# Narrow attention with latents: four evictions and scalings change from VectorE to ScalarE, and GpSimd takes the rows' root ahead of the keys' sum

## The reference, cut to what matters

```python
def mla_attention(x, Wq, Wdkv, Wuk, Wuv, Wo, ln_g, ln_b):
    q = (x @ Wq.T).reshape(b, t, N_HEADS, HEAD_DIM).transpose(0, 2, 1, 3)
    latent = layernorm(x @ Wdkv.T, ln_g, ln_b)
    k = (latent @ Wuk.T).reshape(b, t, N_HEADS, HEAD_DIM).transpose(0, 2, 1, 3)
    v = (latent @ Wuv.T).reshape(b, t, N_HEADS, HEAD_DIM).transpose(0, 2, 1, 3)
    q = apply_rope(q)
    k = apply_rope(k)
    scores = jnp.einsum('bhqd,bhkd->bhqk', q, k) / np.sqrt(HEAD_DIM)
    scores = jnp.where(causal, scores, -jnp.inf)
    attn = jax.nn.softmax(scores, axis=-1)
    out = jnp.einsum('bhqk,bhkd->bhqd', attn, v).transpose(0, 2, 1, 3).reshape(b, t, D_MODEL)
    return out @ Wo.T
x = x + mla_attention(rmsnorm(x, norm1_w), ...)      # x here is a layer norm of the residual
```

## Time and profile before

| | us |
|---|---|
| median of 3 runs (lowest to highest) | 2046.31 (2046.07 to 2053.31) |
| the profiled execution, its own time | 2049.34 |
| its span | 2047.5 |
| busy: TensorE, VectorE, ScalarE, GpSimd | 1493.7, 1348.0, 1172.9, 773.1 |
| mean granted TensorE clock | 0.895 |

### The profile page before, as it was taken

One profiled execution on the slowest core, in us unless ns is written; L12 is line 12 of the kernel. 1 busy time (PEld: TensorE's weight loads), 2 busy tenths in 40 slices (PEclk: granted clock), 3 DMA queues, 4 the chain that ended last, 5 costly groups with the idle time before them and its releaser, 6 DMA issues. The chain is left out here.

```text
span 2047.5 us, 63292 instructions
## 1 busy us (share of the span) xinstructions
PE 1493.7 (73%) x22193; PEld 1111.0 (54%) x22194; DVE 1348.0 (66%) x3733; ACT 1172.9 (57%) x2974; POOL 773.1 (38%) x823
## 2 busy tenths in 40 slices
PE   0688888846888877788424992888888884499991
PEld 0466666624555555556223780566666663377781
DVE  4577777636777777776454664678777875366665
ACT  2366666623544444444433990798888883377770
POOL 0000000022322323231485561336666666466661
PEclk9999999967999999999556995899999996699996
DMA  7110000000001000000012223000011111222227
GB/s 231 32 34 27 31 31 25 26 6 27 31 20 33 21 29 25 26 33 18 23 43 72 74 66 96 12 12 30 29 32 32 31 36 33 79 81 77 81 77 250
DMA packets 110889, 100.81 MB, mean 49 GB/s; under 512 B 17827, under 2 KB 98598, under 8 KB 110656
## 3 DMA queue, kind: packets, MB, share of 16 engines
q1 hardware_dynamic: 87648, 67.02, 11.0%
q0 software_dynamic: 12928, 25.60, 3.8%
q10 hardware_dynamic: 10080, 5.01, 0.8%
HBM read 43.25 MB, written 32.96 MB: 37 GB/s over the span
## 5 line engine op out<-in xcount | busy, mean ns | idle before, releaser
L2497 POOL DMA_INDIRECT e_back<-e_out_rows,e_G x142 | 148.4, 1045 | 98.8 <-issue 56.7
L664 DVE TENSOR_REDUCE m_mx<-m_pM 128x8 f32<-128x1024 f32 x128 | 155.6, 1216 | 29.6 <-PE m_pM L375 29.5
L1459 ACT ACTIVATE w_weights<-w_pS,w_ng 128x77 f32<-128x77 f32 x512 | 157.8, 339 | 17.7 <-DVE w_ng L1547 17.5
L526 ACT ACTIVATE m_PT<-m_pS 128x1024 f32<-128x1024 f32 x128 | 130.4, 1019 | 59.3 <-PE m_pS L404 58.0
L1112 POOL DMA_INDIRECT e_rows<-re_R,re_index x128 | 126.1, 985 | 63.7 <-issue 35.2
L526 ACT ACTIVATE a_PT<-a_pS 77x1024 f32<-77x1024 f32 x128 | 130.5, 1019 | 17.8 <-PE a_pS L404 12.6
L2520 DVE TENSOR_TENSOR e_gl<-e_g,e_gh 128x512 f16<-128x512 f32 x142 | 98.3, 692 | 57.4 <-ACT e_g L2464 53.7
L769 POOL TENSOR_SCALAR a_var<-a_aggr 128x4 f32<-128x4 f32 x16 | 3.1, 193 | 337.0 <-DVE a_aggr L590 337.0
L1660 POOL TENSOR_TENSOR w_weights<-w_weights,w_rec 128x616 f32<-128x616 f32 x64 | 77.9, 1217 | 125.4 <-DVE w_rec L1551 125.0
L664 DVE TENSOR_REDUCE a_mx<-a_pM 128x8 f32<-128x616 f32 x128 | 101.5, 793 | 33.0 <-PE a_pM L375 33.0
L1459 ACT ACTIVATION_READ_ACCUMULATOR w_weights<-w_pS,w_ng 128x1 f32 x512 | 113.6, 222 | 0.0
(11 more groups left out here) (383 smaller groups left out, 5651.1 us busy)
## 6 DMA issues: line engine op xcount, KB each, us to landing
e_G<-e_rows SPq DMA_DIRECT2D x106, 132.0 KB, 2.3
e_B<-e_back SPq DMA_DIRECT2D x16, 512.0 KB, 6.9
stage<-in_split SPq DMA_DIRECT2D x13, 512.0 KB, 4.6
Qs<-a_qh SPq DMA_DIRECT2D x128, 32.0 KB
Qs<-m_qh SPq DMA_DIRECT2D x128, 32.0 KB
Ks<-m_kh SPq DMA_DIRECT2D x32, 128.0 KB
e_R<-e_back SPq DMA_DIRECT2D x16, 256.0 KB, 3.5
w_stage<-in_late SPq DMA_DIRECT2D x16, 256.0 KB, 2.6
```

The lines of the kernel that those rows point to most:

```text
L526: act.activation(PT[:NK, b % 2, 8 * half:8 * half + 8, :], pS[:NK, :, :], ACT.Exp, scale=float(1.0 / np.sqrt(HD))).then_inc(exp_done, 1)
L664: dve.tensor_reduce(out=mx[:, 8 * half:8 * half + 8], in_=pM[:, :, :NK], op=ALU.max, axis=AX.X).then_inc(m_max, 1)
L1459: ac = act.activation(weights[:, b % 2, n, :], pS[:, n // HB, n % HB, :KC], ACT.Exp, bias=ng[:, b % 2, n:n + 1], scale=float(WD) ** -0.5, ...
L2497: pool.indirect_dma_start(out=back, out_offset=bass.IndirectOffsetOnAxis(ap=G[:, r, s, D:D + 1].bitcast(I32), axis=0), in_=out_rows[:, r, ...
```

## The change

Four pieces of work change engine: the scaling of rows by the root (`rms_rows`), the eviction of the values (`part("v")`), gain and bias of the latents (`part("latT")`) and the copy of the turned maxima (`keep_max`). ScalarE used to make `lh` from `lt`; now it makes both from PSUM. On GpSimd the root of the squares stands ahead of the rope of `ks`.

```diff
         @block.scalar
+                elif what == "v" and latent:
+                    act.wait_ge(used, u + 1)
+                    wait(act, pv_ready, lin(g, GB, -GB))
+                    settle(act, c)
+                    for b in range(GB):
+                        cp = act.activation(V[:NK, p, b, :, 0:HD],
+                                            pP[:NK, b * P:(b + 1) * P].rearrange("k (h d) -> k h d", h=H), ACT.Copy)
+                    cp.then_inc(evac, 1)
                 elif what == "latT":
-                    act.wait_ge(evac, u + 1)
-                    act.activation(lh[:], lt, ACT.Copy).then_inc(hi_made, 1)
+                    act.wait_ge(used, u + 1)
+                    wait(act, lat_lo, lin(g, 1, 0))
+                    settle(act, c)
+                    act.activation(lh[:], pP[:LAT, :TG], ACT.Identity, scale=SM("lg", LAT),
+                                   bias=SM("lb", LAT)).then_inc(hi_made, 1)
+                    act.activation(lt, pP[:LAT, :TG], ACT.Identity, scale=SM("lg", LAT),
+                                   bias=SM("lb", LAT)).then_inc(evac, 1)
+            def rms_rows(g):
+                act.wait_ge(ms_done, lin(g, 1, 1))
+                if not is_first(g):
+                    act.wait_ge(lat_lo, lin(g, 1, 0))
+                settle(act, c)
+                for b in range(GB):
+                    act.activation(xn[:, b:b + 1, :], Y[:, bass.ds(lin(g, GB, b), 1), :], ACT.Copy,
+                                   scale=rr[:, b:b + 1]).then_inc(rms_r, 1)
+
+            def keep_max(g, b):
+                act.wait_ge(mt_ready, lin(g, GB, b + 1))
+                wait(act, s_ready, lin(g, 2 * GB, 2 * (b - 1)))
+                act.activation(mT[:, b % 2, :], pTh[:], ACT.Copy).then_inc(mt_kept, 1)
...
             def step(g, p, b, nxt, nxt2):
                 one, two = earlier(g, b, 1), earlier(g, b, 2)
+                if latent:
+                    keep_max(g, b)
                 what, gw, far = slot(b, 0, g, nxt, nxt2)
                 if what:
-                    part(what, gw)
+                    part(what, gw, (p + far) % 2)
                 if two:
                     output_hi(*two)
                 exps(g, p, b, 0)
...
                 if latent and b == 1 and nxt2:
                     squares(shift(g, 2))
+                if latent and b == 2 and nxt2:
+                    rms_rows(shift(g, 2))
...
         @block.vector
-            def rms_rows(g):
-                dve.wait_ge(ms_done, lin(g, 1, 1))
-                if not is_first(g):
-                    dve.wait_ge(lat_lo, lin(g, 1, 0))
-                for b in range(GB):
-                    dve.tensor_scalar(xn[:, b:b + 1, :], Y[:, bass.ds(lin(g, GB, b), 1), :], rr[:, b:b + 1], None,
-                                      ALU.mult).then_inc(rms_r, 1)
...
-                elif what == "v":
+                elif what == "v" and not latent:
...
-                elif what == "latT":
-                    dve.wait_ge(used, u + 1)
-                    wait(dve, lat_lo, lin(g, 1, 0))
-                    dve.tensor_scalar(lt, pP[:LAT, :TG], SM("lg", LAT), SM("lb", LAT), ALU.mult,
-                                      ALU.add).then_inc(evac, 1)
...
-                keep_max(g, b)
+                if not latent:
+                    keep_max(g, b)
...
         @block.gpsimd
                 for half_ in (0, 1):
                     what, gw, far = slot(b, half_, g, nxt, nxt2)
+                    if b == 1 and half_ == 1 and nxt2:
+                        squares(shift(g, 2))
                     if what:
                         rope(what, gw)
-                if b == 1 and nxt2:
-                    squares(shift(g, 2))
```

More of the change, by code:

```diff
@@ L489, in _, with part @@
         def _(act):
-            def part(what, g):
+            def part(what, g, p):
                 u = use(g, what)
@@ L546, in begin @@
                 for what, k in start:
-                    if latent and what == "x" and k == 1:
-                        squares((None, 1))
-                    part(what, (None, k))
+                    if latent and what == "x":
+                        if k == 1:
+                            squares((None, 1))
+                        rms_rows((None, k))
+                    part(what, (None, k), k)
             def step(g, p, b, nxt, nxt2):
                 one, two = earlier(g, b, 1), earlier(g, b, 2)
+                if latent:
+                    keep_max(g, b)
                 what, gw, far = slot(b, 0, g, nxt, nxt2)
                 if what:
-                    part(what, gw)
+                    part(what, gw, (p + far) % 2)
                 if two:
@@ L713, in begin @@
                         norm_rows((None, k))
-                        if latent:
-                            rms_rows((None, k))
                     part(what, (None, k), k)
@@ L740, in step @@
                     norm_rows(shift(g, 2))
-                if latent and b == 2 and nxt2:
-                    rms_rows(shift(g, 2))
                 if more:
```

## The result

The changed kernel is **slower**: 2095.51 us (median of 4 runs, 2092.48 to 2099.77) against 2047.95 for the kernel before beside it (4 runs). The ratio is 1.0229, with an interval of 1.0200 to 1.0259. The profiled execution took 2093.13 us, with a span of 2091.3.

The account below looks back on a forecast made before the run. It took a chain over all four engines as the bound, with neither TensorE nor VectorE full. Profiled 2049.3 + 34.1 for the chain - 3.0 for the profiled run above its median = 2080.4, clock 0; said 2080, range 2052 to 2104.

Parts of the forecast that it names:

- second low clock: Rival, chance 0.15: idle time in step 2 brings TensorE to 1.2 GHz there too; 2080 + 18 = 2098 us.
- The queue of step 2: On ScalarE, the root's delay 1.15, copy of `mT` 0.18 and V copies 0.72 come ahead of `oh`: +2.05 us.
- The turn of x: Step 2: scaling stands behind `keep_heads` on ScalarE, so TensorE turns x at 722.24 in place of 719.91, +2.33 us.
- the predicted 0.22: Step 3: `lh` and `lt` made on idle ScalarE let the next q projection start 0.22 us earlier.
- ScalarE's prices: 128x128 copy from PSUM 0.27, scaling 0.40, `lh` and `lt` 0.78 us each; operand 0.09, overlap 0.09.
- The sum of the chain: Fourteen groups at 2.33 give 32.6; +0.9 without `latT` gain, +1.6 in the start, -1.0 for DMA: +34.1 us.
- The clock: A 1.2 GHz stretch costs 1.3 us; change taken as 0, bounds -13 (all gone), +18 (one more per group).
- The root was not free: Rival, chance 0.07: GpSimd's root lies in its idle time, only 0.9 stays in ScalarE's queue; 18 us slower, 2064.
- VectorE was not the bound: Rival, chance 0.10: VectorE is the bound, ScalarE's waits stay off the path; 1.68 us a group off, 2023.
- Delays weren't covered: Rival that nothing moves, chance 0.05: delays in step 2 are covered by DMA waits in most groups; 2046 to 2052.

Follow-up runs that it names:

- e1: Changed kernel with GpSimd's root of the squares put back behind the rope of `ks`: 2068.04 us, ratio 1.0115 to the kernel before.
- e2: Changed kernel with the V copies (the values' eviction) back on VectorE: 2075.62 us, ratio 1.0149 to the kernel before.
- e4: Changed kernel with the copy of the turned maxima `mT` back on VectorE: 2090.81 us, ratio 1.0216 to the kernel before.
- filled pair: Changed kernel and kernel before, each with unread matmuls put into TensorE's holes to keep its clock up: 2075.41 us and 2043.54 us.
- h1: Changed kernel with GpSimd's root behind the rope of `ks` and the row scaling on VectorE again: 2046.00 us, ratio 1.0009 to the kernel before.
- f3: Kernel before with only the V copies moved to ScalarE: 2047.87 us, ratio 1.0006.
- f2: Kernel before with only GpSimd's root moved ahead of the sum of `ks`: 2054.39 us, ratio 1.0048.
- g3: Kernel before with GpSimd's root between the sum and low part of `ks`, plus unread matmuls in step 3: 2046.14 us, ratio 1.0012.

## Why the prediction was right, and where it was short

The forecast was 2080 (2052 to 2104), slower at 0.85; measured were 2095.5. Direction, mechanism and place were right, and one term was taken at nothing. The measured time is at the upper end of the forecast's own range (2062 to 2095) and inside the stated one because that was drawn wide for the second low clock.

- **The queue of step 2.** `oh` +2.05 predicted, 4.68 - 2.61 = +2.07 in the trace. That it fits to 0.02 is partly luck: the root's part was +1.15 and is 1.29 (e1), V 0.72 and is 0.63 (e2; the copies last 740.74 - 740.12 = 0.62), `mT` in step 2 0.18 and is 0.14 (e4). The root was short because GpSimd began it 0.80 us behind the start of the sines (736.86 - 736.06), and not at 0.62 (714.20 - 713.58).
- **The turn of x.** +2.33 predicted, 8.66 - 6.33 = +2.33 in the trace. In the filled pair ordinary groups are 32.62 and 30.15: +2.47. The other 0.14 fits the copy of `mT` in step 1 (0.18 predicted) with next to nothing gained by `latT` (0.03 for the predicted 0.22).
- **ScalarE's prices**, for which no row existed. Groups by line and shape of the changed kernel (busy us, mean ns; idle before):

```profile
L514 ACT ACTIVATE V<-m_pP 128x128 f32<-128x128 f32 x64 | 12.3, 283 | 0.0
L547 ACT ACTIVATE m_mT<-m_pT 128x128 f16<-128x128 f16 x64 | 17.0, 265 | 11.7 <-PE m_pT L382 11.2
L541 ACT ACTIVATE m_xn<-YW,m_rr 128x128 f32 x40 | 12.6, 389 | 0.0
L521 ACT ACTIVATE m_lh<-m_pP,small 64x512 f16<-64x512 f32 x16 | 12.4, 774 | 26.3 <-PE m_pP L358 26.3
L523 ACT ACTIVATE m_xn<-m_pP,small 64x512 f32<-64x512 f32 x16 | 12.2, 763 | 0.0
```

  A copy from PSUM was taken at 0.27 and is 0.265 to 0.283; the scaling at 0.40 is 0.389, and four last 1.26 for 1.33; `lh` and `lt` at 0.78 are 0.774 and 0.763. Prices from the nearest rows, with the operand's 0.09 and the overlap's 0.09, were good to 6% in the durations and to 0.1 us in what they add to the queue.
- **The sum of the chain.** 34.1 predicted, 31.3 in the filled pair.
- **The clock: the step that failed.** The prediction wrote "I take 0 for the likeliest, as the wait in step 3 stays", with bounds of -13 and +18. It had counted ten groups with a low stretch, all in step 3; `values` shows nine, eight of them in step 3 and one in step 0. The wait in step 3 did stay, and grew (1.71 to 2.45 us in the groups shown); but the clock fell in step 2 as well, behind the new holes, in eight of thirteen groups. Measured: +12.7 us. The prediction's own price gives nearly that: 17 - 9 = 8 more stretches at 1.3 us are 10.4. What spoke against it, three groups with gaps of 1.7 us at full clock, was weak evidence: in step 2 two waits (1.38 and 0.85) stand close together, ahead of the 1.33 before the turn of x, and by e1, e2 and e4 it is the two ahead of `values` together that go with the low clock. So the rival "a second low clock" (0.15) was what happened in over half of the groups, and 2080 + 12.7 - 2.8 = 2090 is what the forecast would have been with both terms as measured, in the place of 2095.5. The other 5 us are no part of the kernel's account: the sum took 3.0 off because the profiled execution before was above its median, and the profiled one of the changed kernel was 2.4 below its own (2093.13 and 2095.51).
- **The other rivals.** The root was not free (e1: 1.29 us a group). VectorE was not the bound: it lost 24.47 - 21.47 = 3.0 us of work a group and nothing came of it, in any of the kernels. Delays weren't covered, though the wait for `Ks` shrank as one would have to expect, from 15.3 us in 14 places to 2.6 in one: it was taken over by longer waits for `ol`.
- **What the prediction didn't see.** It added the pieces one by one. Undone singly they give 3.29 us at the turn of x in place of 2.33; the three that h1 leaves in place cost nothing measurable. With the scaling on VectorE behind `oh` and the sum on time, VectorE has 0.89 us to wait for the root, and a delay of `oh` of 0.63 (f3) or 0.79 (h1) lies in it; the change took that wait away and put the root ahead of `oh` instead. That this is why the singles don't add up is the reading that fits h1, f3 and f2.

## What to carry to other kernels

Before moving work to an engine that is half idle, look at what stands behind it in that engine's queue: ScalarE was busy 15 of 30 us, and yet each of its added copies went into the group's length, because they came between a late input and an instruction on which all four engines hang. The same copies cost nothing where something behind them had to wait longer anyway (f3, h1). A wait that is taken away by reordering is paid by whatever was moved behind: put such work behind the last thing that the chain needs, not ahead of it. And where TensorE gets a new hole, price the clock as its own term, from rows at both levels.

## What the runs showed of the hardware

- The stretches at the low clock went from nine to 17 when TensorE's holes in step 2 went from 0.28 and 1.13 us to 1.38, 0.85 and 1.33, with its work unchanged. The whole cost 12.7 us in the stage, over a quarter of the difference between these two kernels. One hole of 2.25 us in place of the first two did the same (e4: eight groups low in step 2, as with two holes), one of 1.20 to 1.37 did it in two groups (e2), one of 0.85 in none (e1).
- A low stretch costs about 1.0 us in step 2 (9.64 in place of 8.66) and 1.4 in step 3 (10.05 in place of 8.64).
- Holding the clock up with unread matmuls gave the changed kernel 0.66% back by the ratios (1.0229 to 1.0163, 14 us) and 19.4 us in the stage of its profile, and the kernel before nothing that can be told. In g3 they cost the ordinary groups 0.5 us each (29.17 to 29.70).
- In the loop the same group at full clock comes out at 30.15 us time after time, to 0.02 (one group nearer its start has 30.93), while whole executions of one kernel spread over 10 us and more. The structure of a change is read better from such a group than from the median.
